# Attention: in units where VectorE has both, the low part of the probabilities ahead of the maximum of the rough scores

## The reference

```
qkv = (x @ Wqkv).reshape(B, T, 3, H, HD)
q, k, v = (qkv[:, :, 0], qkv[:, :, 1], qkv[:, :, 2])
scores = jnp.einsum('bqhd,bkhd->bhqk', q, k) * jnp.float32(HD) ** (-0.5)
attn = jax.nn.softmax(scores, axis=-1)
out = jnp.einsum('bhqk,bkhd->bqhd', attn, v).reshape(B, T, D)
```

## Time and profile before

| | us |
|---|---|
| median of 3 runs | 1807.43 |
| lowest and highest | 1802.59, 1815.03 |
| the profiled execution | 1807.76 |
| its span | 1806.0 |
| attention in it, first to last unit | about 799 to 1437 |

### The profile page before, as it was taken

One profiled execution on the slowest core, in us unless ns is written; L12 is line 12 of the kernel. 1 busy time (PEld: TensorE's weight loads), 2 busy tenths in 40 slices (PEclk: granted clock), 3 DMA queues, 4 the chain that ended last, 5 costly groups with the idle time before them and its releaser, 6 DMA issues.

```text
span 1806.0 us, 26024 instructions
## 1 busy us (share of the span) xinstructions
PE 1475.8 (82%) x8977; PEld 1371.9 (76%) x8977; DVE 1202.7 (67%) x1777; ACT 930.6 (52%) x1576; POOL 507.3 (28%) x385
## 2 busy tenths in 40 slices
PE   3878859969598849658989899898988798498886
PEld 2756749959598749648878788787888798498786
DVE  6988888515677631157684876848678577687774
ACT  7878544202355322125664646646467622387774
POOL 1000012000002332214453545534357600253332
PEclk9888869979799969859999999999999999699999
DMA  5000021121112341100000000000000197387774
GB/s 162 1 1 1 1 62 44 33 69 51 35 51 86 119 168 38 35 1 18 1 18 0 0 17 0 17 0 0 0 17 27 31 263 199 124 233 218 216 209 120
DMA packets 56015, 121.33 MB, mean 67 GB/s; under 512 B 7264, under 2 KB 23268, under 8 KB 55936
## 3 DMA queue, kind: packets, MB, share of 16 engines
q1 hardware_dynamic: 48448, 98.09, 17.5%
q0 software_dynamic: 7488, 22.26, 5.4%
HBM read 89.57 MB, written 33.70 MB: 68 GB/s over the span
## 4 chain that ended last, share of the span: by engine, by line
PE 27%; DVE 14%; DMA 12%; issue 7%; POOL 2%; ACT 2%; DVEq 0%; SPq 0%; POOLq 0%; ACTq 0%
DMA out_dram<-yrow,index 11%; DVE mcol L884 5%; PE ps L331 5%; PE ps L332 5%; PE ps L333 5%; DVE rz L893 4%; PE ps L686 3%; DVE prlo L854 2%; PE ps L725 2%; PE ps L706 2%; PE ps L727 1%; PE ps L708 1%; PE ps L726 1%; POOL prlo L854 1%; PE ps L695 1%
## 5 line engine op out<-in xcount | busy, mean ns | idle before, releaser
L854 POOL TENSOR_TENSOR prlo<-prob,prhi 125x500 fp32r<-125x500 f32 x180 | 255.8, 1427 | 370.5 <-ACT prob L818 370.5
L816 ACT ACTIVATE prhi<-ps 125x500 fp32r<-125x500 f32 x300 | 177.5, 592 | 122.2 <-PE ps L708 112.0
L884 DVE TENSOR_REDUCE mcol<-ps 125x1 f32<-125x1250 f32 x120 | 174.4, 1454 | 32.8 <-PE ps L686 32.2
L725 PE MATMUL ps<-prhi,vhi 125*128 125x250 f32 x600 | 172.7, 288 | 25.4 <-POOL prlo L854 12.9
L854 DVE TENSOR_TENSOR prlo<-prob,prhi 125x500 fp32r<-125x500 f32 x120 | 121.6, 1014 | 92.7 <-ACT prob L818 91.7
L818 ACT ACTIVATE prob<-ps 125x500 f32<-125x500 f32 x300 | 176.8, 589 | 3.1 <-DVE prlo L854 3.0
L727 PE MATMUL ps<-prlo,vhi 125*128 125x250 f32 x600 | 169.1, 282 | 0.0
L726 PE MATMUL ps<-prhi,vlo 125*64 125x250 f32 x600 | 168.1, 280 | 0.0
L706 PE MATMUL ps<-qst,kst 128*125 128x250 f32 x600 | 157.7, 286 | 4.8 <-ACT q L808 3.9
L1392 PE MATMUL ps<-ohs,ohd 128*125 128x417 bf16 x380 | 118.7, 399 | 50.0 <-DVE ohs L1828 50.0
L708 PE MATMUL ps<-q,k 128*125 128x250 f32 x600 | 155.5, 282 | 0.0
(11 more groups left out here) (301 smaller groups left out, 4054.0 us busy)
## 6 DMA issues: line engine op xcount, KB each, us to landing
w2st<-in_L_ffn_W_dram SPq DMA_DIRECT2D x27, 1152.0 KB, 6.1
w1all<-in_L_ffn_W_dram SPq DMA_DIRECT2D x8, 1152.0 KB, 11.7
wqst<-in_L_ffn_Wqkv_dram SPq DMA_DIRECT2D x12, 384.0 KB, 4.0
hid_d<-tin SPq DMA_DIRECT2D x10, 375.0 KB
tin<-hid_d SPq DMA_DIRECT2D x10, 375.0 KB
vtin<-xn_d SPq DMA_DIRECT2D x10, 375.0 KB
out_dram<-accr POOLq DMA_DIRECT2D x10, 375.0 KB, 8.3
xall<-in_x_dram SPq DMA_DIRECT2D x5, 672.0 KB
```

The lines of the kernel that those rows point to most:

```text
L725: pe.matmul(ps[:, b:b + GQ], vhi[:, e, kt, :], hi, start=kt == 0, stop=False)
L816: act.activation(prhi[:, n % RING, :], bank(3 + n % 3, P, 2 * GQ), ACT.Exp, scale=float(HD) ** -0.5)
L854: eng.tensor_tensor(prlo[:, n % RING, :], prob[:, n % 3, :], prhi[:, n % RING, :].bitcast(f32), ALU.subtract)\
L884: dve.tensor_reduce(mcol[:, e, t:t + 1], ps[0:P, 0:N], AX.X, ALU.max, negate=True).then_inc(sem("max"), 1)
```

## The change

In `head` on DVE, a unit's low part is now issued first and the maximum of the rough scores second. Units that have only one of the two are as before. The two meet at units 11, 13, 21 and 23 of each first half and at 6, 8, 16 and 21 of each second half except the last, which prepares no other.

```diff
             def head(p, e, other):
                 for j in range(UNITS):
+                    if not by_pool(j):
+                        lower(dve, p, e, j, "pr_lo")
                     if other is not None and j in ROUGH_AT[e]:
                         maximum(*other, ROUGH_AT[e].index(j))
-                    if not by_pool(j):
-                        lower(dve, p, e, j, "pr_lo")
                     if j in OUT_AT[e]:
                         outputs(p, e, OUT_AT[e].index(j))
```

## The result

The median of 22 runs is 1820.76 us, against 1811.71 us of 22 runs of the kernel before. The ratio is 1.0049 with a 95% interval of 1.0032 to 1.0066: +8.9 us, between +5.8 and +12.0. The profiled execution has a span of 1821.1 us against 1806.0. Forecast were +8.9 us, and with them 1816 us, from a median before of 1807.4 over three runs; over 22 runs that median is 1811.7, so 4.3 of the 4.8 us by which the time lies above 1816 are the base's. What follows shows that two terms of the sum were wrong, and that a third thing, left out of it, made up for them: the agreement of the total is luck.

The account below looks back on a forecast made before the run. TensorE in attention, never out of work, waits briefly, mostly rough products on DVE's maxima (26.3 us). Terms 0.35 + 1.1 + 2.9 + 4.5 = +8.9 us upon the profiled 1807.8 give 1816.7, median 0.3 lower: 1816; eight-in-ten range 1803 to 1823.

Parts of the forecast that it names:

- first half, units 11 and 13, pairs 0 to 4: Exchanges beside POOL's long `wqlo`: +0.85 us per pair if POOL goes first, about -1.1 if DVE does; sum +0.35.
- first half, units 21 and 23, pairs 0 to 4: M9 starts 0.25 us later in each pair, holding up the maxima's transposition and the next projection.
- first half, pair 5: POOL's `wplo` keeps out lo11, leaving +1.1 us at R6, and lo21, making M8, R9 and M9 1.65 later.
- second halves: Exchanges at units 6, 8, 16 and 21 delay M9 and the next start by 0.9 us per pair, five times: +4.5.
- The disputed term: Who gets the port at lo11, pairs 0 to 4: POOL first in 1, 2, 4, DVE in 0, 3; +0.35 us.
- the case that I gave 0.25: Rival, chance 0.25: DVE gets the port ahead of POOL's `wqlo` in every pair, giving 1810 us.
- The row that I set against it: DVE's `lo` of 1102.37 went first (0.66 us) though POOL's `vlo` started 0.23 us earlier; cited against POOL first.
- The handover at unit 6: Second halves: POOL's waiting `lo` goes first when `k2` ends, lo6 takes about 1.7 us, R1 starts 1.0 later.
- Unit 16: Second halves: lo16 takes 0.67 us ahead of M5 instead of 1.28 behind it, making R6 0.45 later.
- Unit 21: Second halves: the exchange makes R9 another 0.45 us later and M9 another 0.3.
- The clock: Rival, chance 0.10: longer waits at the ends of both halves drop TensorE to half clock; +23 us, 1830.
- The signs that I had named: Profile after: lo11 3.9 us with `wqlo` ahead, lo6 about 1.7, lo16 and lo21 0.67, loop turn 113 to 114 us.

## Why the prediction was right in its sum and not in all its steps

| step | forecast | measured at full clock |
|---|---|---|
| first half, units 11 and 13, pairs 0 to 4 | +0.35 | -4.75 |
| first half, units 21 and 23, pairs 0 to 4 | +1.25 | +1.2 |
| first half, pair 5 | +2.75 | +2.75 |
| second halves | +4.5 | +6.05 |
| half clock | 0 | +4.9, the rest of the five profiles' +10.1 |
| sum | +8.9 | +10.1 by five profiles, +8.9 (5.8 to 12.0) by the times |

- *The disputed term failed* in its step "I take POOL first in pairs 1, 2 and 4". DVE went first in all five, the case that I gave 0.25 and priced at -1.1 each; it measured -0.95. The row that I set against it (0.23 us behind and still first) was the better witness. I had taken one row of each kind; the same trace has 13 low parts of DVE that start 0.20 to 0.23 us behind a record of POOL, of which 7 went first and 6 were held, so the chance of 0.25 was too low for a lag of half that. The Trainium skill's rule in "SBUF — State Buffer", "Who interferes with whom" (the first to start holds the pair for the whole instruction), holds here for the holding, as 4.11 against 3.48 us and 2.54 us show; for who starts first the record's start does not tell it to 0.1 us, nor to 0.3, as the last section shows.
- *Second halves* had the right mechanism and too small a size. The handover at unit 6 and the 0.25 left at M2 came as forecast (0.15). Unit 16 measured 0.6 for a forecast 0.45: M5 starts a whole low part later (0.60), and R6 waits for it alone. Unit 21 had 0.6 at R9, and M9 kept 0.36 of it (0.3).
- *First halves, units 21 and 23, and the last pair* came out to a tenth, all from rows: which POOL instruction is running when the low part comes.
- *The clock* I had as a rival for a loss over 1%, and left out of the sum. Three more stretches came with the change in its first profile and five in its second. What it is worth, 4.9 us, is a difference: the phases' lengths less the order's 5.25. Counted stretch by stretch instead, each half against the same half at full clock, the stretches cost 5.0 and 7.8 us in the two profiles of the change and 0.7, 3.0 and 1.6 in the three of before, 4.6 between the means. That the exchanges at units 16 and 21 bring the stretches in second halves is shown by the table; that the longer waits for R6 and R9 do it (1.9 us instead of 1.3) is argued only, since no kernel with the same exchange and shorter waits was run.
- So an error of -5.1 us at the disputed place met one of +1.55 in the second halves and one of +4.9 in the clock. With the right winner of the race and the clock still left out, my sum would have been 3.0 us, well below the 5.8 to 12.0 that the times allow; even the order's true price, 5.25, lies just below them.
- *The signs that I had named* came out mixed. lo6 (1.72 us), lo16 and lo21 (0.68) of second halves are as named, and the turn of the loop, from M3 to M3, is 113.0 us in the mean against 111.4 before. lo11 of 3.9 us did not appear. R6 and R9 are later in second halves, but R6 is about 1 us earlier in first halves at full clock. And one sign of being wrong did appear: half-clock stretches at more than two pairs' starts, three in the first profile of the change and four in the second.

The same clock takes back what first halves gain: with a half-clock stretch at the keys' split, M2 is 0.53 late and lo11 meets another instruction of POOL (0.99 us), so that the gain of 0.9 at M5 is gone. It was so in pairs 1 and 2 of the change's first profile; in pair 4, where lo11 took 0.73 us behind such a stretch, 0.25 of the gain was left.

## What to carry to other kernels

When an instruction's duration in a trace varies fourfold, ask first what another engine holds at that moment: moving it by a microsecond can be worth more than its own length, and the whole of an exchange can have places of either sign. Price such a change place by place and keep only the ones that gain; here one of the eight places, alone, is faster than both kernels. And where an engine is nearly always busy, an order that makes its waits half a microsecond longer may cost as much again in its clock: the exchange at units 16 and 21 cost 4.8 us by its places and 4.5 more in the length of the phase. Count the stretches at half clock in more than one profile before a sum is called explained.

## What the runs showed of the hardware that I had not expected

- With POOL's record 0.10 to 0.11 us ahead, DVE's instruction on two SBUF tensors went first and POOL's took 4.1 us instead of 3.5; at 0.21 us POOL had gone first, at 0.23 us once more DVE. Over all 13 profiles of this case, low parts of DVE that start 0.20 to 0.25 us behind a record of POOL are of both kinds, 58 ahead and 47 held; in four rows of pair 5 DVE went first even 0.32 to 0.33 us behind (0.66 us, POOL's `wplo` 2.7 instead of 1.84), and from 0.34 us on every one was held. So the start of a record on POOL does not tell who goes first; what decides it no run shows.
- Every low part of DVE that was held, in all 13 profiles, ended 0.53 to 0.54 us behind the end of POOL's record.
- An instruction that waits for the port goes ahead of the next one of the engine that had it: lo6 took 1.71 to 1.72 us behind `k2` in every second half of the change that has this exchange, in both profiles.
- Two profiles of one kernel agree within 0.06 us at the places compared here at full clock, and differ by 1 to 3 us in the phase; the difference is that of the half-clock stretches.
